# First attention of a four-layer kernel on one core: probabilities made with keys on partitions, the maximum alone by query

## The chip, the cores and the metric

One core of a Trainium2 chip runs the whole program in one launch. The metric is the device time of a launch in microseconds (us), the median of the runs shown. The engines have queues of their own and meet by semaphores: PE (matrix products, which land in PSUM, eight banks of 512 float32 per partition), DVE (vector work), ACT (activations and copies), POOL (GpSimd) and SP (issues most of the DMAs).

## What is computed

Four blocks in a row on x of 4 x 1024 x 256, each added to x behind a gate: a cross attention, a mixture of 16 experts, a second attention, and a quantised linear layer. The change is in the first block alone:

```python
def _L0_xattn_ref(q_in, mem, mem_mask, Wq, Wk, Wv, Wo):
    q = _split_heads(q_in @ Wq.T)          # 16 heads of 16
    k = _split_heads(mem @ Wk.T)           # 64 keys for each of 4 batches
    v = _split_heads(mem @ Wv.T)
    scores = jnp.einsum('bhqd,bhkd->bhqk', q, k) / jnp.sqrt(jnp.float32(D_HEAD))
    scores = jnp.where(mem_mask, scores, -jnp.inf)
    attn = jax.nn.softmax(scores, axis=-1)
    out = jnp.einsum('bhqk,bhkd->bhqd', attn, v)
    ...
    return out @ Wo.T

x = x + jnp.tanh(g_xattn[0]) * _L0_xattn_ref(_layernorm(x, axis=-1), ctx_1024, mask_Bx1x1xS2_bf1, ...)
```

## The kernel before

The program has stages, with a barrier between them. A setup stage loads x (4 MB, kept in SBUF as `x_sb`) and the weights, makes the keys of all batches (`kT_sb`), spreads them to `kbd`, where the keys of eight heads stand beside each other with zeros for the other heads' rows, and the values to `vbd`.

The first attention then runs over eight chunks of 512 queries (two per batch), each of four tiles of 128 queries. In a chunk PE transposes the normalised x (`x0`, `x1`), makes the queries in two halves of 128 rows (`q0`, `q1`), and the scores of each tile: 128 queries by 16 heads times 64 keys, 1024 columns in two PSUM banks. The mask is added there by a one-pass bf16 product (L651) before the float32 product (L653). DVE takes the maximum over the keys (L574) and subtracts it (L576) into `probs` in SBUF; ACT takes the exponential (L521); DVE sums it (L582) and takes the reciprocal (L585); POOL multiplies (L474). PE transposes the probabilities back, so that keys lie on partitions: eight pairs of heads `pt0` to `pt7` (L661), which ACT moves to `probT`. Then come the values (L679, four products of 32 columns at a time, each in its own 32 columns of PE's array), whose result `oT` ACT moves, and the output projection (L689), which DVE adds to x (L591).

The chunks are software pipelined: beside the probabilities of chunk c PE makes the queries and scores of chunk c + 1, in an order written out by hand in `body`. Every engine executes its own list in order. Scores use banks 0 to 3, two for each tile in turn. Everything else goes through a ring of banks 4 to 7: a product may start when the product four places earlier in the ring has been moved out (`Ring.free`). Beside the attention the weights of two experts per chunk are loaded and split into a high part (ACT, L506 and L507) and a low part (DVE, L563 and L565) for the next stage. `ln_vector` (L215 to L227) normalises chunk c + 2 ahead.

## Time and profile before

| what | value |
|---|---|
| median of 3 runs | 1526.14 us (1525.16 to 1529.63) |
| span of the profiled execution | 1543.6 us |
| own time of the profiled execution beside it | only its span is given, 17.5 us above the median of the runs |
| busy: PE, DVE, ACT, POOL | 1113.8, 1014.9, 637.1, 486.5 us |
| mean granted PE clock | 0.848 of 2.4 GHz |
| setup / first attention / all that follows | 0 to 27.65 / 27.65 to 241.65 / 241.65 to 1543.6 us |

Busy time is what an engine's instructions cover; the shares over the whole span mix stages with different limits, so a change in one stage is read from that stage's own stretch of the trace. Idle time is put down to what released the engine.

### The profile page before, as it was taken

The numbers are of one execution on the slowest core, as the hardware profiler recorded it, in microseconds if no ns is written. First come the engines' busy times: TensorE is split into PE (matmuls) and PEld (weight loads), VectorE is DVE, ScalarE is ACT, GpSimd is POOL, SyncE is SP. The second block draws the span as 40 slices with busy tenths as digits, with TensorE's granted clock in tenths as the row PEclk, the third lists the DMA queues.
The fourth block names the chain that finished last, engine by engine and source line by source line (L and its number), as shares of the span: only waits on it lengthen the run. The fifth ranks groups of instructions, "written<-read, shape, count | busy, mean of one in ns | idle before, by whom it ended". The sixth has DMA issues, their size and how long they took to land. (4 is left out here: it accounts for less than half of the span.)

```text
span 1543.6 us, 23798 instructions
## 1 busy us (share of the span) xinstructions
PE 1113.8 (72%) x8155; PEld 569.9 (37%) x8155; DVE 1014.9 (66%) x1856; ACT 637.1 (41%) x1280; POOL 486.5 (32%) x539
## 2 busy tenths in 40 slices
PE   3799985342407999805465568999999999998757
PEld 2355553121204666502232323333333333331646
DVE  4899985455453766525556387888888888870665
ACT  0455553111102333201122207777677767775430
POOL 1243341767760000078777061111111111111110
PEclk7999997656657999956767759999999999995988
DMA  6001100222259999943656431111211121100003
GB/s 204 22 21 42 41 1 14 89 85 86 91 200 214 250 258 259 244 122 89 210 182 196 143 101 40 55 38 39 59 54 38 39 59 53 38 2 1 1 0 109
DMA packets 183649, 146.24 MB, mean 95 GB/s; under 512 B 102638, under 2 KB 160494, under 8 KB 183546
## 3 DMA queue, kind: packets, MB, share of 16 engines
q1 hardware_dynamic: 162570, 102.61, 25.3%
q0 software_dynamic: 12288, 33.57, 6.7%
q10 hardware_dynamic: 8688, 8.66, 1.7%
q8 instruction: 68, 1.11, 0.3%
q14 instruction: 35, 0.29, 0.1%
HBM read 53.11 MB, written 68.55 MB: 79 GB/s over the span
## 5 line engine op out<-in xcount | busy, mean ns | idle before, releaser
L1782 DVE TENSOR_REDUCE small<-ps 128x2 f32<-128x960 f32 (+6 forms) x384 | 379.0, 1040 | 56.8 <-PE ps L1837 56.5
L1761 ACT ACTIVATE region<-ps 128x512 f32<-128x512 f32 (+5 forms) x768 | 343.1, 532 | 110.0 <-PE ps L1851 108.6
L1732 POOL TENSOR_SCALAR_AFFINE_SELECT region<-region 128x512 f32<-128x512 f32 (+2 forms) x160 | 87.7, 548 | 427.4 <-ACT region L1761 427.4
L1851 PE MATMUL ps<-region 50*128 50x512 f16 (+5 forms) x896 | 198.6, 332 | 26.7 <-ACT region L1761 23.7
L1927 PE MATMUL ps<-region 128*32 128x512 f32 (+5 forms) x1792 | 192.9, 504 | 2.0 <-POOL region L1732 1.5
L1200 PE MATMUL ps<-region 128*128 128x384 f16 x696 | 125.2, 331 | 38.8 <-DMA region<-expert_rows 38.0
L859 POOL DMA_INDIRECT expert_rows<-region,small x128 | 130.6, 1020 | 65.1 <-issue 36.6
L1837 PE MATMUL ps<-region 48*128 48x480 f16 (+6 forms) x896 | 141.4, 333 | 13.5 <-DVE small L1782 11.3
L1365 POOL DMA_INDIRECT region<-result_rows,home x128 | 133.5, 1043 | 38.0 <-issue 36.8
L1851 PEld LDWEIGHTS ps<-region 50*128 50x128 f16 (+1 forms) x896 | 54.2, 95 | 211.3 <-ACT region L1761 195.6
L1200 PEld LDWEIGHTS ps<-region 128*128 x696 | 67.6, 99 | 83.5 <-issue 45.5
L474 POOL TENSOR_TENSOR region<-region,small 128x1024 f32<-128x1024 f32 x32 | 61.0, 1917 | 118.4 <-DVE small L585 118.4
L1523 PE MATMUL ps<-region 128*128 128x512 f16 (+1 forms) x240 | 62.7, 435 | 42.0 <-DVE region L1462 32.8
L1436 DVE SCALAR_TENSOR_TENSOR x_sb<-region,weights,x_sb 128x256 f32<-128x256 f32 x128 | 52.1, 477 | 52.4 <-DMA region<-result_rows,home 52.4
L1082 DVE SCALAR_TENSOR_TENSOR region<-ps,region 128x384 f32<-128x384 f32 x58 | 32.3, 558 | 74.4 <-ACT region L902 74.3
L1832 PE MATMUL ps<-small 64*128 64x128 bf16 (+1 forms) x768 | 68.8, 245 | 17.0 <-POOL small L1713 11.9
L902 ACT ACTIVATE region<-ps 128x384 f32<-128x384 f32 x58 | 28.5, 491 | 122.2 <-PE ps L1200 122.2
L1213 PE MATMUL ps<-region 128*128 x522 | 67.4, 275 | 2.5 <-DVE region L1094 2.5
L1837 PEld LDWEIGHTS ps<-region 48*128 48x128 f16 x896 | 49.1, 97 | 51.3 <-DVE small L1782 47.2
L653 PE MATMUL ps<-region,small 128*128 128x512 f32 x128 | 65.4, 592 | 0.0
L1353 POOL MEMSET small<- 128x1 f32 x1 | 0.1, 101 | 204.0 <-POOLq L778 204.0
L1094 DVE COPY region<-ps 128x768 f32<-128x768 f32 x58 | 55.0, 947 | 3.4 <-PE ps L1213 3.4
(237 smaller groups left out, 1693.3 us busy)
## 6 DMA issues: line engine op xcount, KB each, us to landing
result_rows<-region SPq DMA_DIRECT2D x58, 384.0 KB, 4.1
region<-v_parts SPq DMA_DIRECT2D x16, 576.0 KB, 4.1
v_parts<-region SPq DMA_DIRECT2D x14, 576.0 KB
region<-k_parts SPq DMA_DIRECT2D x96, 68.0 KB, 2.2
region<-q_parts SPq DMA_DIRECT2D x96, 64.0 KB, 2.1
k_parts<-region SPq DMA_DIRECT2D x16, 272.0 KB
x_sb<-in_x ACTq DMA_DIRECT2D x8, 512.0 KB, 9.1
region<-in_w13T SPq DMA_DIRECT2D x16, 256.0 KB, 3.0
```

The costliest lines, as they stand in the source:

```text
L653: ins = nc.tensor.matmul(o, qT[:, m, j * P:(j + 1) * P], kbd[:, m, bass.ds(b, 1), :].rearrange("p a n -> p (a n)"), start=False, stop=True)
L859: nc.gpsimd.indirect_dma_start(out=xs, out_offset=bass.IndirectOffsetOnAxis(ap=sloti[:, b, at_:at_ + 1], axis=0), in_=rows[:, b, j, :], in ...
L1200: ins = nc.tensor.matmul(ps[:, 2 * (g % DEEP) + half_, 0:GROUP], w, xgT[:, g % G_BUFS, part, kh, :], start=n == 0, stop=n == 5)
L1213: ins = nc.tensor.matmul(ps[:, 6 + j // 2, (j % 2) * D:(j % 2 + 1) * D], (hgh, hgl)[part][:, g % DEEP, j * P:(j + 1) * P], flat((w2h, w2l) ...
L1365: nc.gpsimd.indirect_dma_start(out=yg[c % 2][:, j, r, :], out_offset=None, in_=ys, in_offset=bass.IndirectOffsetOnAxis(ap=home[:, c, at_:a ...
L1732: nc.gpsimd.affine_select(out=t, in_=t, compare_op=ALU.is_ge, fill=0.0, base=r0, pattern=[[0, G], [1, w]], channel_multiplier=-1).then_inc ...
L1761: nc.scalar.activation(dst, src, ACT.Exp, scale=SCALE).then_inc(s_exp, 1)
L1782: nc.vector.tensor_reduce(nmp[:, qt, :, p0:p0 + np_, place], s_pair(n + first)[:, :, 0:np_ * nk] .rearrange("p e (h k) -> p e h k", h=np_) ...
L1832: nc.tensor.matmul(o, mask_id[rows[half], part, :], mask_dg[rows[half], part, 0:np_, :], start=part == 0, stop=False, skip_group_check=True)
L1837: ins = nc.tensor.matmul(banks[half][:, p * nk:(p + 1) * nk], q_of(r, v)[:, p0 + p, qt * P:(qt + 1) * P], k_of(r, v)[:, p0 + p, k0:k0 + nk ...
L1851: ins = nc.tensor.matmul(o, k_of(rr, tbuf)[:, pair, kt * P:kt * P + rows], q_of(rr, tbuf)[:, pair, q0:q0 + nq], start=True, stop=True)
L1927: ins = nc.tensor.matmul(ps[32 * h:32 * h + 32, O_BANK, q0 - hf * CH:q0 - hf * CH + nq], vg[0:rows, buf, (kt * G + h) * 32:(kt * G + h + 1 ...
```

## The change

The probabilities are no longer made by query and transposed. The scores by query stay, without a mask, and serve the maximum alone (`largest`). The masked-out keys are replaced by the mean of the kept ones in the setup, so that they can't raise the maximum. The negated maximum is cut into two bf16 parts (`shift_parts`), transposed by PE (`shifts`, the product `n`) and moved by ACT to `negT`. Then PE makes the scores a second time with keys on partitions (`scores_by_key`): for each of eight pairs of heads one bf16 product that spreads the shift over the 128 keys of the pair, and one float32 product of 32 rows of keys with 32 rows of queries on top. Four pairs use the four groups of 32 rows of the array and four banks. ACT takes the exponential out of PSUM straight to `probT`, with the mask as its bias. After the values, PE sums the probabilities over the keys (`row_sums`), DVE takes the reciprocal of all 512 sums of 16 heads at once (a 128x256 tile), PE spreads it over the head's 16 rows (`spread_out`), and DVE multiplies the output with it (`normalise`). POOL's multiplication and the transposes of probabilities are gone. `Turns` replaces `Ring`: one list of 20 products a chunk over the same four banks, the same rule of four places. POOL makes the constants for this in the setup.

The core of the diff:

```diff
-                order.mark(nc.vector.memset(maskb[:], 0.0))
...
+                order.mark(nc.vector.tensor_tensor(kT_sb[:], ps[:, 0:KH, 0:B * CTX],
+                                                   keep[:].unsqueeze(1).to_broadcast([P, KH, B * CTX]), ALU.mult))
+                order.wait()
+                order.mark(nc.vector.tensor_reduce(mean[:], kT_sb[:].rearrange("p m (b k) -> p m b k", b=B), AX.X, ALU.add))
...
+                st = [((f"st{a}", c), "act") for a in range(PAIRS_OF)]
+                tail = [(("ov0", c), "act"), (("ov1", c), "act"), (("sum", c), "dve"), (("r0", c), "dve"), (("r1", c), "dve"),
+                        (("o0", c), "dve"), (("o1", c), "dve")]
+                return x + st[0:4] + q[0:1] + st[4:8] + q[1:2] + tail + ([(("n", c + 1), "act")] if ahead else [])
...
+                def exp(c, a):
+                    act.wait_ge(s_full, turns.full((f"st{a}", c)))
+                    nc.scalar.activation(probT[:, a, :], ps[:, turns.bank((f"st{a}", c)), :], ACT.Exp, scale=SCALE,
+                                         bias=mbias[:, c // 2:c // 2 + 1]).then_inc(s_act, 1)
...
-                    nc.vector.tensor_tensor(probs[h][:, j, :].rearrange("p (h k) -> p h k", k=CTX), s3,
-                                            nmx[:, j, :].unsqueeze(2).to_broadcast([P, H, CTX]),
-                                            ALU.add).then_inc(s_shift, 1)
...
+                def reciprocals(c):
+                    dve.wait_ge(s_full, turns.full(("sum", c)))
+                    nc.vector.reciprocal(recip[:], ps[:, turns.bank(("sum", c)), 0:QH]).then_inc(s_dve, 1)
+
+                def normalise(c, m):
+                    dve.wait_ge(s_act, turns.moved((f"ov{m}", c))[1])
+                    dve.wait_ge(s_full, turns.full((f"r{m}", c)))
+                    nc.vector.tensor_tensor(oT[:, m, :], ps[:, turns.bank((f"r{m}", c)), :], oT[:, m, :], ALU.mult).then_inc(s_dve, 1)
...
+                def scores_by_key(c, pairs):
+
+                    wait_moved("n", c)
                     for a in pairs:
...
+                        m, r = a // 4, slice(32 * (a % 4), 32 * (a % 4) + 32)
+                        wait_free(f"st{a}", c)
+                        nc.tensor.matmul(slot(f"st{a}", c), shift_of[r, m, :], negT[r, :], start=True, stop=False)
+                    for a in pairs:
+                        m, g = a // 4, a % 4
+                        r = slice(32 * g, 32 * g + 32)
+                        nc.tensor.matmul(slot(f"st{a}", c), kbd[r, m, c // 2, P * g:P * g + P], qT[r, m, :],
+                                         start=False, stop=True).then_inc(s_full, 1)
...
+                def row_sums(c):
+
+                    wait_free("sum", c)
+                    for g in range(4):
+                        for m in range(KH):
+                            for qh in range(2):
+                                k = 2 * m + qh
+                                ins = nc.tensor.matmul(slot("sum", c)[32 * k:32 * k + 32, 0:QH], sum_of[:, g, :],
+                                                       probT[:, 4 * m + g, qh * QH:(qh + 1) * QH], start=g == 0, stop=g == 3)
...
+                    scores_by_key(c, range(4))
+                    if ahead:
+                        queries(c + 1, 0)
+                    scores_by_key(c, range(4, 8))
+                    if ahead:
+                        queries(c + 1, 1)
+                    if ahead:
+                        scores(c + 1, 0)
+                        scores(c + 1, 1)
+                    values(c, 0)
+                    values(c, 1)
+                    row_sums(c)
+                    if ahead:
+                        scores(c + 1, 2)
+                    spread_out(c, 0)
+                    spread_out(c, 1)
+                    if ahead:
+                        scores(c + 1, 3)
+                    outputs(c)
+                    if ahead:
+                        shifts(c + 1)
```

PE's list for the middle of a chunk before, from the queries of the next chunk on (L642 queries, L661 transposed probabilities, L651 and L653 mask and scores; what an instruction waits for stands in brackets):

```order
L642 MATMUL ps<-small 128x512 [waits a_act_moved,a_dve_moved]
L642 MATMUL ps<-small 128x512
L642 MATMUL ps<-small 128x512 [waits a_dve_moved]
L642 MATMUL ps<-small 128x512
L661 MATMUL ps<-ident,region 128x128 [waits a_prob,a_act_moved]
L661 MATMUL ps<-ident,region 128x128 [waits a_prob] x3
L661 MATMUL ps<-ident,region 128x128 [waits a_act_moved]
L661 MATMUL ps<-ident,region 128x128 x3
L651 MATMUL ps<-maskb,onesb 128x512 [waits a_shifted,a_act_moved]
L653 MATMUL ps<-region,small 128x512
```

The two halves of the queries follow each other, and eight transposes stand between the second half and the first scores. Now, in the same place of a chunk (L756 shift products, L760 key products, L728 query halves, L738 scores):

```order
L756 MATMUL ps<-region 128x512 [waits a_act_moved] x3
L760 MATMUL ps<-small,region 128x512 x4
L728 MATMUL ps<-small 128x512 [waits a_act_moved]
L728 MATMUL ps<-small 128x512
L756 MATMUL ps<-region 128x512 [waits a_act_moved] x4
L760 MATMUL ps<-small,region 128x512 x4
L728 MATMUL ps<-small 128x512 [waits a_act_moved]
L728 MATMUL ps<-small 128x512
L738 MATMUL ps<-region,small 128x512 [waits a_maxed,a_act_moved]
```

The query halves stand apart, each behind a group of key products, and every group, half and the first scores begin with a wait for a move by ACT. DVE's list for one chunk, between the low parts of the expert weights and the additions to x, before:

```order
L574 TENSOR_REDUCE small<-ps 128x16
L576 TENSOR_TENSOR region<-ps,small 128x1024
L582 TENSOR_REDUCE small<-region 128x16
L585 RECIPROCAL small<-small 128x16
L574 TENSOR_REDUCE small<-ps 128x16
```

and now:

```order
L639 TENSOR_REDUCE small<-ps 128x16 [waits a_scores] x2
L657 RECIPROCAL region<-ps 128x256 [waits a_bank_full]
L639 TENSOR_REDUCE small<-ps 128x16 [waits a_scores]
L662 TENSOR_TENSOR small<-ps,small 128x512 [waits a_bank_full,a_act_moved] x2
L639 TENSOR_REDUCE small<-ps 128x16 [waits a_scores]
L648 CAST region<-small 128x2x4x2 [waits a_maxed]
```

Of the three instructions on a whole tile one is left; the reciprocal of the chunk's sums and the two products with it have come between the maxima. After the last chunk, the low parts of two experts now stand behind the additions to x instead of ahead of them.

## Rows read from the trace of the kernel before

**Rows 1.** Busy times by stage: stretch, its length, busy PE, PEld, DVE, ACT, POOL, clock, DMA.
```profile
27.65:61.86 34.21, 21.08 (x52) 9.72 (x53) 24.65 (x48) 8.61 (x13) 11.52 (x13) 0.75 0.19 58
61.86:227.28 165.42, 153.38 (x721) 90.74 (x719) 147.92 (x233) 93.32 (x156) 59.06 (x38) 1.00 0.10 29
227.28:241.65 14.37, 11.49 (x61) 8.94 (x61) 4.64 (x7) 5.87 (x10) 1.32 (x1) 0.77 0.00 1
```

**Rows 2.** The same view, one chunk of the seven.
```profile
85.21:108.89 23.68, 22.07 (x105) 13.12 (x104) 21.61 (x36) 13.25 (x22) 8.58 (x6) 1.00 0.11 34
```

**Rows 3.** Groups by line, 37 to 232 us: count, busy us, mean ns of one.
```profile
L576 DVE TENSOR_TENSOR region<-ps,small 128x1024 f32<-128x1024 f32 x32 | 39.2, 1224 | 1.1
L574 DVE TENSOR_REDUCE small<-ps 128x16 f32<-128x1024 f32 x32 | 39.0, 1218 | 9.8 <-PE ps L653 9.6
L582 DVE TENSOR_REDUCE small<-region 128x16 f32<-128x1024 f32 x32 | 38.3, 1197 | 0.0
L563 DVE SCALAR_TENSOR_TENSOR region<-region 128x512 f16<-128x512 f32 x17 | 13.4, 790 | 5.4 <-ACT region L507 5.4
...
L565 DVE SCALAR_TENSOR_TENSOR region<-region 128x256 f16<-128x256 f32 x17 | 8.8, 518 | 0.0
...
L585 DVE RECIPROCAL small<-small 128x16 f32<-128x16 f32 x32 | 8.1, 253 | 1.1
```

**Rows 4.** PE's timeline in one chunk: start us, busy us of the merged instructions, line.
```profile
108.37 3.70 PE L642 MATMUL ps<-small 128*128 128x512 f32 x8 [1.60 <-DVE x_sb L591]
111.91 1.04 PE L661 MATMUL ps<-ident,region 128*128 128x128 f32 x8
112.78 0.38 PE L651 MATMUL ps<-maskb,onesb 128*128 128x512 bf16 x1
113.00 1.02 PE L653 MATMUL ps<-region,small 128*128 128x512 f32 x2
113.86 0.38 PE L651 MATMUL ps<-maskb,onesb 128*128 128x512 bf16 x1
...
121.94 1.93 PE L679 MATMUL ps<-region,small 128*32 128x512 f32 x16
123.80 0.39 PE L651 MATMUL ps<-maskb,onesb 128*128 128x512 bf16 x1
```

**Rows 5.** Timeline: moves by ACT in the first, a middle and the last chunk.
```profile
40.57 0.60 ACT L511 ACTIVATE small<-ps 128x512 f32<-128x512 f32 x1 [1.66 <-PE ps L642]
...
110.39 0.60 ACT L511 ACTIVATE small<-ps 128x512 f32<-128x512 f32 x1 [2.94 <-PE ps L642]
...
118.92 2.04 ACT L511 ACTIVATE region<-ps 128x512 f32<-128x512 f32 x4
...
236.49 0.60 ACT L511 ACTIVATE small<-ps 128x512 f32<-128x512 f32 x1 [0.29 <-PE ps L679]
...
237.13 3.72 PE L689 MATMUL ps<-small 128*128 128x256 f32 x16 [0.71 <-ACT small L511]
```

**Rows 6.** PE's timeline in the second attention: two products of 50 rows, and one.
```profile
1010.05 0.39 PE L1851 MATMUL ps<-region 50*128 50x512 f16 x2
...
1011.19 0.39 PE L1851 MATMUL ps<-region 50*128 50x512 f16 x1 [0.20 <-ACT region L1761]
```

**Rows 7.** Groups by line over the whole span, other stages.
```profile
L2003 ACT ACTIVATE region<-ps,gambet 128x512 f32<-128x512 f32 x16 | 11.7, 774 | 30.0 <-PE ps L2092 30.0
...
L1807 DVE TENSOR_TENSOR region<-ps,small 128x512 f32 x14 | 9.7, 691 | 2.0 <-DVE small L1805 0.2
...
L1805 DVE RECIPROCAL small<-ps 128x32 f32<-128x32 f32 x16 | 5.7, 358 | 48.1 <-PE ps L1887 48.1
```

**Rows 8.** DVE's timeline in the setup.
```profile
18.45 1.70 DVE L372 CAST maskb<-small 1x256 bf16<-1x256 f32 x8
```

**Rows 9.** Busy times in the last chunk, columns as in rows 1.
```profile
223.60:227.00 3.40, 1.10 (x7) 0.68 (x5) 3.33 (x6) 2.49 (x5) 2.16 (x2) 1.00 0.00 0
227.00:230.40 3.40, 1.90 (x9) 1.74 (x9) 3.40 (x5) 0.98 (x2) 1.60 (x1) 0.50 0.00 0
```

More of the change, by code:

```diff
@@ L112, in free, with __init__, bank, full @@
         return e, c * self.by.count(e) + self.moved_before[e] - self.previous[at:].count(e) + 1
+class Turns:
+    def __init__(self, items, banks):
+        self.place = {key: i for i, (key, _) in enumerate(items)}
+        assert len(self.place) == len(items)
+        self.by = [e for _, e in items]
+        seen = {}
+        self.counted = []
+        for e in self.by:
+            seen[e] = seen.get(e, 0) + 1
+            self.counted.append(seen[e])
+        self.banks = banks
+    def bank(self, key):
+        return self.banks[self.place[key] % len(self.banks)]
+    def full(self, key):
+        return self.place[key] + 1
+    def moved(self, key):
+        i = self.place[key]
+        return self.by[i], self.counted[i]
+    def free(self, key):
+        i = self.place[key] - len(self.banks)
+        return (self.by[i], self.counted[i]) if i >= 0 else None
 def hold(eng, sem, n, tick):
@@ L397, in flamingo @@
         oT = view(small, "oT", [P, KH, CH], F32)
[L398 to L401 removed]
+        nmx = view(small, "nmx", [P, TC, KH, 4, 2], F32)
         junk = view(small, "junk", [P, 4], F32)
@@ L495, in _ @@
                                         pattern=[[1, P]], channel_multiplier=-1).then_inc(s_const, 1)
-                normalise(0, 0)
-                chunks(pool, body)
+                for c in range(CHUNKS - 2):
+                    ln_pool(nc.gpsimd, c + 2, s_var, s_rstd)
             @block.scalar
             def _(act):
-                credit(nc.scalar.activation(junk[:, 1:2], half[:, 0:1], ACT.Copy), s_act, CREDIT)
                 def high(k, at_, n):
@@ L543, in _, with move @@
-                move_queries(ring_first, 0)
-                for j in range(TC):
-                    exp(0, 0, j)
-                high(*SHARED)
-                chunks(act, body)
-                for expert in experts_beside(1, B - 1):
-                    high(*expert)
-                move_probs(ring_last, 0)
-                move_outputs(ring_last, 0)
+                def move(name, c, dst):
+                    act.wait_ge(s_full, turns.full((name, c)))
+                    nc.scalar.activation(dst, ps[:, turns.bank((name, c)), :], ACT.Copy).then_inc(s_act, 1)
@@ L592, in add @@
                                                        in1=xt, op0=ALU.mult, op1=ALU.add).then_inc(s_dve, 1)
-                def softmax(c, h, order):
-                    shift(c, h, 0, order)
-                    for j in range(1, TC):
-                        shift(c, h, j, order)
-                        row_sum(c, h, j - 1, order)
-                    row_sum(c, h, TC - 1, order)
-                FIRST, EACH = 2 * LN_MARKS + 2 * TC, LN_MARKS + 2 * TC
-                def body(c, h, b, b_next, more):
-                    order = Order(dve, s_self, c * EACH + FIRST)
-                    if more:
-                        ln_vector(nc.vector, order, c + 2, 1e-5, s_var, s_rstd, s_xn, free=(s_full, ring.full(c, "x1")))
-                    for expert in experts_beside(h, b):
-                        low(expert)
-                    softmax(c + 1, 1 - h, order)
-                    add(ring, c, c)
@@ L617, in _ @@
+                shift_parts(0)
                 low(SHARED, signal=False)
-                chunks(dve, body)
-                for expert in experts_beside(1, B - 1):
+                for c in range(CHUNKS):
+                    ahead = c + 1 < CHUNKS
+                    if c + 2 < CHUNKS:
+                        ln_vector(nc.vector, order, c + 2, 1e-5, s_var, s_rstd, s_xn, free=(s_full, turns.full(("x1", c + 1))))
+                    if c:
+                        for expert in experts_beside((c - 1) % 2, (c - 1) // 2):
+                            low(expert)
+                    if ahead:
+                        largest(c + 1, 0)
+                        largest(c + 1, 1)
+                    reciprocals(c)
+                    if ahead:
+                        largest(c + 1, 2)
+                    normalise(c, 0)
+                    normalise(c, 1)
+                    if ahead:
+                        largest(c + 1, 3)
+                        shift_parts(c + 1)
+                    add(c)
@@ L709, in _ @@
-                queries_of(pe_first, 0, 0)
-                pe_first.wait_moved(0, "q1")
-                for j in range(TC):
-                    scores(0, 0, j)
-                chunks(eng, body)
-                transposed_probs(pe_last, 0, CHUNKS - 1, 1)
-                values(pe_last, 0)
-                outputs(pe_last, 0)
+                        ins.then_inc(s_full, 1)
+                transposed(0)
+                for m in range(KH):
+                    queries(0, m)
+                for j in range(TC):
+                    scores(0, j)
```

340 lines of the change are left out of this document (186 added, 154 removed).

## The prediction

> **What bounds the kernel now.** I read the busy times by stage first. The change touches the setup, up to 27.65 us, and the first attention, 27.65 to 241.65 us [rows 1]; the other 1302 us run the same code. In the attention's middle, 61.86 to 227.28 us, PE is busy 153.4 of 165.4 us and DVE 147.9: both are nearly full, ACT and POOL are not. Cut into chunks, that stretch is seven periods, nearly all of 23.68 us [rows 2].
>
> Then I read the groups by line. The three DVE instructions on a whole 128x1024 tile cost 1.2 us each [rows 3], four of each per chunk: 4 x (1.22 + 1.22 + 1.20) = 14.6 us, with normalisation, split weights and the rest making up the 21.6 us of DVE in a chunk [rows 2].
>
> Then PE's timeline for one chunk, where distances between starts say what an instruction costs the queue [rows 4]. Eight 128-column transposes take 112.78 - 111.91 = 0.87 us. A 512-column product of one-pass bf16 takes 113.00 - 112.78 = 0.22, and a float32 one, issued as two passes, 113.86 - 113.00 = 0.86. Eight float32 products of 32 columns each take 123.80 - 121.94 = 1.86, not 8 x 0.86: four run side by side, so two rounds are 1.72, and 0.14 is left for changing the array's division. A chunk's PE work before is then 0.87 (x) + 3.44 (queries) + 3.48 (32 transposes of probabilities) + 1.73 (mask) + 6.88 (scores) + 1.72 (values) + 3.44 (outputs) = 21.6 us.
>
> **The change: work.** DVE loses L576 and L582 with their small reciprocals, 4 x (1.22 + 1.20 + 0.25) = 10.7 us a chunk [rows 3]. It gains a reciprocal of 128x256, which no row shows. Sixteen columns take 0.253 us [rows 3] and 32 take 0.358 [rows 7], so 6.6 ns a column: 0.358 + 224 x 0.0066 = 1.83 us (bounds: 0.36 if width were free, 2.9 in proportion). It gains two 128x512 products from PSUM at 0.69 [rows 7] and eight 16-element instructions, taken as 0.85 us together (bounds 0.4 to 2.0, eight at 0.25). DVE falls to about 15 of 23.7 us. POOL's 1.9 us normalisations go too. ACT keeps about its load: eight moves and four 1024-wide exponentials become eight 512-wide exponentials. Each reads its bias from a tile: with two such operands an ACTIVATE takes 0.774 us against 0.60 [rows 5, 7], so one adds 0.09.
>
> PE loses 3.48 + 1.73 = 5.2 us a chunk and gains four bf16 transposes (0.25), two groups of four shift and four key products, row sums (32 passes of 256 columns, four side by side: 1.72) and spreading (four float32 products of 256 columns: 1.72). The groups use 32 of the 128 rows. Two tiles of 50 rows do run side by side: two 512-column products take 0.39 us, as one does [rows 6]. So I take four as one, 0.22 + 0.86 a group; no row shows four. Sum 0.25 + 2.16 + 1.72 + 1.72 = 5.85: **PE does not get lighter, it goes from 21.6 to 22.2 us a chunk.**
>
> The Trainium skill, TensorE: Matmul & The Clock Gate, Part 3 (Packing small matmuls), measures only 3.07 times for four tiles of 32 rows and 512 columns. My estimate from that page: 0.33 us more a group, 0.65 a chunk, 5 us in all; the sum would be 1564 instead of 1559.
>
> **The change: order.** This decides. PE executes strictly in the written order, and the new ring hands each of banks 4 to 7 on after four products: the first query half needs the bank of st0, the fourth shift of the second group needs that query half moved, the second query half needs st4's bank. None of these has other PE work in front of it. The turnarounds come from the rows: from the end of a product's issue to ACT's start 0.30 (108.37 + 1.72 to 110.39) [rows 4, 5]; to DVE taken the same; an ACT move 0.60 and 0.04 more until PE starts (236.49 + 0.60 to 237.13); back-to-back moves 0.48 apart (four in 2.04) [rows 5].
>
> One chunk, from the end of issue of the shift transposes (0): shift moved and both x moved by ACT, 0.30 + 2 x 0.48 + 0.64 = 1.90; fourth shift and key products +1.08 = 2.98; exponential of st0 +0.30 + 0.73 = 4.01; first query half +0.14 + 1.72 = 5.87; moved +0.94 = 6.81; fourth shift and key products +1.08 = 7.89; exponential of st4 +1.03 = 8.92; second query half +1.86 = 10.78; moved +0.94 = 11.72; two scores +3.44 = 15.16; values and row sums +0.14 + 3.44 = 18.74; reciprocal +0.30 + 1.83 = 20.87 (a score lies beside it); spreading +1.72 = 22.6; the last score +1.72 = 24.3; outputs +3.44 = 27.8; next shift transposes +0.25 = **28.0 us against 23.68**. PE waits some 5.7 us of it. The last maximum and the parts of the shift (1.2 + 0.85) and both normalisations hide behind outputs and score; without that cover they would cost up to 2.4.
>
> **Ends of the stage.** In setup the mask's casts (1.70 [rows 8]) and two more instructions go; means, masking of keys and eight small instructions come: +1.6 us on DVE's path (bounds 0 to 4). POOL's 24 small instructions lie beside it, and the two extra loads on SP's queue are small and needed late; uncovered they would cost 2 us. Chunk 0's queries were moved at 41.17 [rows 5]; now 42.8, four scores 6.9, last maximum 1.5, parts 0.85, transposes 0.25: the first chunk starts at 52.3. Seven periods: 248.3. The last chunk has no next one beside it: shift 0.94, first group 1.08, four exponentials 2.8, second group 1.08, four exponentials 2.8, second values 1.0, row sums 1.72, reciprocal 2.13, spreading 1.72, normalising 1.0, outputs 3.44, add 1.1, and now behind it DVE's halves of two experts (0.79 + 0.52 each [rows 3], those overlapping, so 2 x 1.1): 23.0. End at 271.3 instead of 241.65: **+30 us**. For the first and last chunk's clock (below) I add 3, as an estimate between 0 and 7: **+33**.
>
> This is summed on the profiled execution (span 1543.6 us, 17.5 above the runs' median of 1526.14) and carried over unscaled; 1.1% of 33 does not matter. **Forecast 1559 us.** A measurement of this kernel can tell about 0.3% (4.6 us) from no change.
>
> **The rivals.**
> - **No side-by-side for four tiles.** For it: only two tiles are seen, in 16-bit types. Against: eight-pass groups of four column tiles work in float32. Each group's key products would be 3.43 us; the first exponential starts under them, so the query half moves from 4.01 to 5.6: +1.6 a group, 3.2 a chunk, with the ends 24: 1583.
> - **PE's clock falls in the chunks.** In the last chunk before, PE was busy 1.1 us in 223.6 to 227.0, and the next stretch ran at 0.50, the level of 1.2 GHz [rows 9]. Now the stretches 0 to 4 and 5.9 to 8.9 of every chunk hold about 2 and 1.1 us of PE issue. Against: a wait of 1.60 us in each chunk before [rows 4] left it at 1.00 [rows 2]. If one query half and a group in most chunks run at half speed, +3 each, +21: 1580.
> - **Faster: PE's waits vanish, its work bounds.** If other work covered every hand-over between PE and ACT, the period would be PE's 22.2, and the stage would end at 52.3 + 155.4 + 23.0 = 230.7, 11 us earlier: 1515. It decides where a period falls under (241.65 - 52.3 - 23.0) / 7 = 23.8 us, so where 4.2 of the 5.7 us of waits are covered. For it: DVE, the other full engine, is relieved. Against: the written order has nothing to put there.
> - **Nothing.** With 1.5 us of wait a chunk instead of 5.7 the period is 23.8 and the time 1526; nothing in the rows points there.
>
> **How the numbers follow.** Forecast 0.66, no side-by-side 0.11, clock 0.14, faster 0.05, nothing 0.04. Slower is the sum of the first three, 0.91. The forecast's own range is 1541 (small unknowns at their low ends, clock full) to 1573. The range reaches to the two slower rivals: 1541 to 1584; left out are the last two cases and the upper tails, together under 0.2.
>
> **What would show it.** Right: periods of 28 us; DVE about 60% busy and waiting for PE; PE waiting about 1 us before each query half, fourth shift and first score, released by ACT; reciprocal near 1.8. Wrong: periods under 24; four key products over 3 us apart; a reciprocal that PE does not wait for; a clock below 1.0 in the chunks.

## The result, and the profile after

| kernel | median of the runs (us) | range |
|---|---|---|
| before | 1525.65, 4 runs | 1523.53 to 1529.63 |
| after | 1560.12, 4 runs | 1558.95 to 1560.95 |

The ratio is 1.0228, with a 95% interval of 1.0202 to 1.0254: slower, by 34.5 us, where 33 were forecast. The profiled execution of after took 1558.95 us, its span 1557.1.

The whole program's busy times of after, from its page:

```profile
PE 1130.9 (73%) x8379; PEld 561.6 (36%) x8379; DVE 962.3 (62%) x1850; ACT 613.8 (39%) x1255; POOL 427.3 (27%) x527
```

DVE is busy 53 us less than before. PE is busy 17 us longer, which is no measure of its work: after's busy time in a chunk, 24.9 us, exceeds the whole period of the reordered run (below), which has the same products. The stages answer to [rows 1, 2]. Busy times by stretch, with the columns of rows 1: the setup, the start, a middle chunk, the last one, and all behind the stage:

```profile
0.00:34.95 34.95, 7.23 (x40) 5.18 (x40) 11.52 (x43) 1.49 (x2) 10.62 (x38) 0.74 0.54 170
34.95:58.75 23.80, 16.38 (x36) 7.18 (x37) 12.70 (x40) 3.21 (x6) 3.28 (x8) 0.73 0.28 84
141.02:168.44 27.42, 24.89 (x135) 12.40 (x133) 15.39 (x35) 10.45 (x19) 1.01 (x1) 1.00 0.09 29
250.70:276.40 25.70, 17.62 (x100) 8.25 (x97) 9.13 (x14) 8.28 (x15) 0.00 (x0) 0.80 0.00 1
276.40:1557.10 1280.70, 915.49 (x7283) 454.16 (x7283) 826.44 (x1532) 527.68 (x1099) 407.38 (x475) 0.84 0.38 104
```

Every one of the seven chunks takes 27.42 us, where a chunk took 23.68. DVE's share of it is 15.4 us. The stage ends at 276.40 instead of 241.65: +34.75, close to the timed 34.5 (+33.7 against the second profile of before, which ends it at 242.74). One thing does not fit: what follows the stage took 1280.7 us here and 1302 in the profile of before, with the same code. A second profile of before settles that.

### The profile page after: what moved, and what is told of

Read it like the earlier page. It is cut to its first block and busy times, and to the rows that moved or that the text cites. A ratio compares the mean times of both kernels' runs of the same rounds, so it can differ in the third digit from the quotient of the medians.

```text
span 1557.1 us, 24292 instructions
## 1 busy us (share of the span) xinstructions
PE 1130.9 (73%) x8379; PEld 561.6 (36%) x8379; DVE 962.3 (62%) x1850; ACT 613.8 (39%) x1255; POOL 427.3 (27%) x527
## 3 DMA queue, kind: packets, MB, share of 16 engines
q1 hardware_dynamic: 163256, 102.64, 25.1%
## 5 line engine op out<-in xcount | busy, mean ns | idle before, releaser
L1482 POOL DMA_INDIRECT region<-result_rows,home x128 | 129.7, 1013 | 38.0 <-issue 36.3
L265 POOL TENSOR_TENSOR rstd<-ve,half 128x4 f32<-128x4 f32 x24 | 24.6, 1026 | 221.1 <-DVE ve L255 203.4
L639 DVE TENSOR_REDUCE small<-ps 128x16 f32<-128x1024 f32 x32 | 39.2, 1224 | 67.4 <-PE ps L738 66.5
L738 PE MATMUL ps<-region,small 128*128 128x512 f32 x128 | 60.1, 604 | 5.5 <-ACT small L583 5.5
```

The source lines that it names most:

```text
L1482: nc.gpsimd.indirect_dma_start(out=yg[c % 2][:, j, r, :], out_offset=None, in_=ys, in_offset=bass.IndirectOffsetOnAxis(ap=home[:, c, at_:a ...
```

## The experiments

All stage ends and periods in this section are read from the traces: a period is the distance between the starts of two chunks' output products, the end is that of the last DVE instruction of the stage.

| kernel | period | stage end | median us | ratio to before (95%) |
|---|---|---|---|---|
| before, second profile | 23.68 | 242.7 | 1524.45, 16 runs | |
| after | 27.42 | 276.4 | 1560.12 | 1.0228 (1.0202 to 1.0254) |
| no column loads | 27.42 | 275.6 | 1557.58 | 1.0244 (1.0184 to 1.0303) |
| maximum from upper halves | 24.20 | 251.2 | 1535.06 | 1.0081 (1.0045 to 1.0116) |
| reordered | 23.83 | 250.0 | 1532.17 | 1.0063 (1.0036 to 1.0090) |
| other setup | 27.42 | 265.6 | 1549.11 | 1.0184 (1.0127 to 1.0241) |
| all together | 22.00 | 225.9 | 1504.85 | 0.9872 (0.9816 to 0.9927) |
| one more chunk in flight | 20.94 | 218.4 | 1502.63 | 0.9867 (0.9813 to 0.9920) |
| the same, scores ahead of outputs | 20.86 | 218.3 | 1503.23 | 0.9882 (0.9821 to 0.9944) |
| before with its gates late | 23.68 | 238.0 | 1518.46 | 0.9975 (0.9943 to 1.0007) |

Each ratio is taken to runs of before made in the same session, whose medians were 1524.45 (16 runs), 1525.91 (7 runs: other setup, all together, one more chunk) and 1524.03 us (13 runs: the last two rows); it isn't the quotient of the medians shown.

For every kernel the median, less the stage end and the 1.9 us by which a run exceeds its span, leaves 1277 to 1283 us for what follows the stage (1277 in all together), so the stage explains the differences to within some 3 us. Single executions spread more there (1270 to 1283 in these profiles), which is why the medians are compared.

### Before, profiled again

No edit.

> The kernel before once more, for a second profile of it. The changed kernel's attention stage ends 34.7 us later than in the first profile of before (276.4 against 241.65 us), its runs are 34.5 us longer at the median, but its profile is only some 13.5 us longer. Theory: the stage alone grew, and the first profile of before spent about 20 us too many behind the stage; then the stage ends at 241 to 242 us again, what follows it takes 1281 us (plus or minus 4) instead of 1302, and the span is 1522 to 1526 us. Rival: the change also made something behind the stage 20 us faster; then what follows the stage takes about 1302 us again.

Measured: span 1525.5, run 1527.28 us. Busy times of this second execution of before, columns as in rows 1:

```profile
242.74:1525.50 1282.76, 912.74 (x7283) 453.81 (x7283) 826.31 (x1532) 527.58 (x1099) 408.52 (x475) 0.84 0.38 104
```

What follows the stage takes 1282.8 us, the 1281 of the theory within its 4 us. The change touched the first attention and the setup alone; the 1302 us of the first profile were that one execution's.

### The mask's column loads

```diff
-                for dup in range(2):
-                    sp.dma_start(mcol[64 * dup:64 * dup + CTX, :], mask.rearrange("b s -> s b"),
-                                 allow_slow_non_contiguous=True).then_inc(s_mask, 16)
-                dve.wait_ge(s_mask, 48)
+                dve.wait_ge(s_mask, 16)
-                nc.vector.tensor_scalar(mbias[:], mcol, -1.0, 3.0e38, ALU.add, ALU.mult)
+                nc.vector.memset(mbias[:], 0.0)
```

The setup of after is 7.3 us longer than before's. SP's issues in it, from the timeline (start, time to issue, line, target):

```profile
2.87 1.41 SPq L346 DMA_DIRECT2D small<-in_mask  x2
4.31 3.06 SPq L349 DMA_DIRECT2D small<-in_wqT  x1
```

In before the same weight took 0.39 us to issue:

```profile
2.76 0.39 SPq L303 DMA_DIRECT2D small<-in_wqT  x1
```

ACT's timeline, its eight loads of x, in after and then in the second profile of before:

```profile
3.26 18.06 ACTq L362 DMA_DIRECT2D x_sb<-in_x  x8
```

```profile
3.25 12.61 ACTq L316 DMA_DIRECT2D x_sb<-in_x  x8
```

The DMA view of after up to 35 us: the first line is the rate in 40 slices of 0.875 us, then two groups of loads with their size and the time from issue to landing:

```profile
GB/s 0 0 3 120 272 279 329 79 9 5 28 145 191 207 82 165 273 315 379 384 365 346 349 349 348 351 345 349 289 241 117 70 0 0 0 0 0 0 0 0
...
small<-in_wqT SPq DMA_DIRECT2D x1, 256.0 KB, 13.1
...
small<-in_mask SPq DMA_DIRECT2D x2, 0.2 KB, 10.8
```

Right behind the mask's loads the rate falls from 329 to 5 GB/s. The Tanh on ACT stands behind the loads of x, and DVE's whole chain behind the Tanh: it starts at 22.88 instead of 17.43. The column loads move 4 bytes in each of 64 partitions, twice.

> The changed kernel without the two column loads of the mask (one byte per partition); the bias of the exponentials is set to zero by a memset instead, so the mask's bias is left out. Theory (these two loads hold up the queues in the first 20 us, so that the x tiles and the weights come late): DVE's chain over the keys starts 5.4 us earlier, near 17.5 us instead of 22.9, the first chunk starts 5.5 us earlier, and the time falls by 5.5 us to 1554.6. Rival A (the row of the mask sent to all partitions is what blocks): no change, 1560. Rival B (the start is bound by TensorE at half clock, not by DVE): the chain starts earlier but the first chunk moves by less than 1.5 us, 1559.

Measured: 1557.58 us, 2.5 less than after. DVE's first instruction, the first chunk's transposes, and a stretch of busy times (columns as in rows 1), from three views of this run:

```profile
19.56 0.40 DVE L439 TENSOR_SCALAR boutb<-boutb,tg 128x256 f32<-128x256 f32 x1 [19.56 <-ACT tg L362]
```

```profile
55.06 1.04 PE L718 MATMUL ps<-ident,xn 128*128 128x128 f32 x8
```

```profile
57.80:61.20 3.40, 2.86 (x10) 0.84 (x3) 1.38 (x4) 2.21 (x4) 0.85 (x1) 0.50 0.00 0
```

Neither theory nor rival alone. The two column loads are 3.3 of the 5.4 us (22.88 to 19.56). The other 2.1 us are left when only the row sent to 128 partitions remains: the loads of x now take 14.74 us to issue, and 12.68 when that row goes too (the other setup, below). The rate still falls, from 310 to 91 GB/s, in the same slices. The profiles' counts of packets on the largest queue, which carries the loads that SP issues, agree: 163256 in after, 162712 here, 162570 in before, so the column loads are 544 packets and the row 142.

The first chunk begins 3.7 us earlier (58.75 to 55.06), but the stage ends only 0.8 us earlier. From the first chunk's start to its outputs it took 26.49 us, in after 23.75: here PE's clock stood at 0.50 in part of it, where after had 1.00. So 2.7 of the 3.7 us were lost in the first chunk, at the lower clock. These readings rest on the traces: the medians lie only 2.5 us apart, and the runs of the two kernels overlap.

### The maximum from half the bits

```diff
-nc.tensor.matmul(ps[...], qT[:, m, j * P:(j + 1) * P], kbd[:, m, c // 2, :],
+nc.tensor.matmul(ps[...], qT_top[:, m, j * P:(j + 1) * P], kbd_top[:, m, c // 2, :],
+        kbd_top = kbd[:].bitcast(BF16).rearrange("p m b (k two) -> p m b k two", two=2)[:, :, :, :, 1]
```

`qT_top` is the same view of `qT`. Only the maximum sees these scores; it is subtracted in the exponent and divided out again, so it need not be the exact one.

> The changed kernel with the scores for the maximum made from the upper halves of the F32 numbers, read as BF16: one pass through TensorE instead of four, 0.43 us instead of 1.71 for each of the four pairs of a chunk, 5.1 us of TensorE's work a chunk; the other products keep all their bits. Theory (the chain of handovers sets the period): the two pairs ahead of the values lie on the chain (-2.6 us), the third lies beside the reciprocal and gains nothing, the fourth gives 0.5 us until the normalising ends; period 27.42 - 3.1 = 24.3 us, first chunk's start 2 us earlier, last chunk unchanged, time 1560 - 7 x 3.1 - 2 = 1536. Rival A (TensorE's own work of 24.9 us, as its busy row says, sets the period): -5.1 us a chunk, period 22.3, time 1522. Rival B (reading every second BF16 costs as much as the passes saved): 1560.

Measured: period 24.20 (theory 24.3), 1535.06 us (theory 1536). PE's timeline of a chunk from its first two pairs of scores (L740) on:

```profile
166.27 1.08 PE L740 MATMUL ps<-region,small 128*128 128x512 bf16 x4 [0.69 <-ACT small L585]
167.28 1.92 PE L770 MATMUL ps<-region 128*32 128x512 f32 x16
169.02 1.91 PE L781 MATMUL ps<-region 128*32 128x256 f32 x32
...
172.90 1.96 PE L790 MATMUL ps<-region 128*128 128x256 f32 x8 [1.41 <-DVE region L659]
...
175.72 0.48 PE L800 MATMUL ps<-small 128*128 128x256 f32 x1 [0.40 <-DVE small L664]
```

The chain forecast each pair. The first two take 167.28 - 166.27 = 1.01 us where after spends 3.63 (below): -2.6. The third gives nothing: from row sums to spreading it is 172.90 - 169.02 = 3.88 us, to the hundredth as in after (161.25 - 157.37), only that PE now waits 1.41 us for the reciprocal where it had a score to do. The fourth gives 0.7: from spreading to outputs it is 175.72 - 172.90 = 2.82 us, in after 3.52. Of 5.1 us of work removed, 3.2 came out of the period: a path, not a sum of work. The period shows this, not the total, in which the ends moved too. The first chunk began 3.6 us earlier (2 were forecast) and needed the same 23.7 us to its outputs, at a clock of 0.50 to begin with. The last chunk, from the outputs before it to its own, took 20.35 us instead of 22.97, where no change was forecast.

### The same instructions, reordered

```diff
-                    if ahead:
-                        transposed(c + 1)
+                    if ahead:
+                        scores(c + 1, 0)
                     scores_by_key(c, range(4))
-                    if ahead:
-                        queries(c + 1, 0)
+                    if ahead:
+                        scores(c + 1, 1)
                     scores_by_key(c, range(4, 8))
-                        queries(c + 1, 1)
-                        scores(c + 1, 0)
-                        scores(c + 1, 1)
+                        scores(c + 1, 2)
                     values(c, 0)
                     values(c, 1)
                     row_sums(c)
                     if ahead:
-                        scores(c + 1, 2)
+                        scores(c + 1, 3)
+                    if further:
+                        transposed(c + 2)
                     spread_out(c, 0)
                     spread_out(c, 1)
-                    if ahead:
-                        scores(c + 1, 3)
+                    if further:
+                        queries(c + 2, 0)
+                        queries(c + 2, 1)
                     outputs(c)
```

ACT's and DVE's lists and the ring follow; a second buffer holds the queries made a chunk earlier.

> The changed kernel with all its instructions, in another order on TensorE: the queries of a chunk are made a chunk earlier into a second buffer, and the four pairs of scores for the maximum stand where TensorE waits: one behind the transposes of the shift, one behind each group of key products, one behind the row sums, and the next transposes and queries beside the reciprocal and the normalising. Theory (the period of 27.42 us is 22.2 us of work and 5.2 us of waits for ACT and DVE): all but some 0.8 us of the waits are covered, period 23.0 us; the first part is 5 us longer (a second set of queries ahead of chunk 0), six periods of 23.0, a seventh without queries of 18.7 and a last chunk of 22 us put the stage's end at 63.8 + 138 + 18.7 + 22 = 242.5 us, time 1526. Rival A (TensorE's work is the 24.9 us that its busy row shows): period 25 us, stage end 256, time 1539. Rival B (ACT or DVE sets the pace): period 27, time 1560 or more.

Measured: period 23.83, 1532.17 us. Busy times of a middle chunk, then, from PE's timeline, its two key groups (L752 shifts, L756 keys) and the scores (L734) behind each:

```profile
151.42:175.24 23.82, 23.63 (x133) 12.38 (x132) 15.22 (x34) 10.56 (x19) 1.00 (x2) 1.00 0.11 34
```

```profile
156.96 0.40 PE L752 MATMUL ps<-region 32*128 32x512 bf16 x4
157.19 1.03 PE L756 MATMUL ps<-small,region 32*128 32x512 f32 x8
158.14 1.99 PE L734 MATMUL ps<-region 128*128 128x512 f32 x4
160.06 0.46 PE L752 MATMUL ps<-region 32*128 32x512 bf16 x3
160.72 0.39 PE L752 MATMUL ps<-region 32*128 32x512 bf16 x1 [0.19 <-ACT region L592]
...
161.89 1.98 PE L734 MATMUL ps<-region 128*128 128x512 f32 x4
```

Not an instruction fewer, and 3.6 us less a chunk: at least that much of the 27.42 us was waiting. PE is now busy 23.63 of 23.82 us, with one visible wait of 0.19. But its busy row can't be read as work: in after it showed 24.89, more than this whole period, and so rival A's reading of it falls. Starts tell more. The first key group takes 158.14 - 156.96 = 1.18 us, the second, with its wait, 161.89 - 160.06 = 1.83. So some 0.65 us is waiting and about 23.2 are work, an estimate. The theory holds in its mechanism, and its work term of 22.2 was too small: a group takes 1.18 where 1.08 were taken, a pair of scores 1.82 to 1.92 (158.14 to 160.06, the next product being one of 32 rows) where 1.72 were, the row sums 1.84 for 1.72. The stage ends at 250.0, not at 242.5. This order alone did not beat before, whose period was 23.68.

### Another setup

```diff
-                sp.dma_start(mrow, mask.rearrange("b s -> (b s)").partition_broadcast(P)).then_inc(s_mask, 16)
+                sp.dma_start(mrow[0:1, :], mask.rearrange("b s -> (b s)").unsqueeze(0)).then_inc(s_mask, 16)
+                nc.tensor.matmul(ps[:, 6, 0:B * CTX], onesb[:], mask0[:], start=True, stop=True).then_inc(s_all, 1)
-                dve.wait_ge(s_gate, 5 * 16 + 1)
-                order.mark(nc.vector.tensor_scalar(boutb[:], boutb[:], tg[:, 1:2], None, ALU.mult))
...
+                order.mark(nc.vector.tensor_copy(keep[:], ps[:, 6, 0:B * CTX]))
...
+                dve.wait_ge(s_gate, 5 * 16 + 1)
+                order.mark(nc.vector.tensor_scalar(boutb[:], boutb[:], tg[:, 1:2], None, ALU.mult))
```

`mask0` holds the mask's row in its first partition and zeros elsewhere. The excerpt leaves out the bias column and POOL's selects that were moved.

> The changed kernel with another setup and the same chunks: the mask is loaded as one row into one partition (as before the change) and sent to all partitions by one product with ones on TensorE, the bias column is cut out of it on VectorE, VectorE begins with the keys instead of waiting for the gates' Tanh, and 12 of POOL's 20 selects stand in the attention stage. Theory (the setup is bound by VectorE's chain, which the mask loads made late): the chain of VectorE starts near 9 us instead of 22.9, the setup ends with the last x tile at some 23.3 us instead of 35.0, and the stage ends 11.7 us earlier; time 1560 - 11.7 = 1548. Rival A (as the run without the column loads suggests, what the start gains is given back by TensorE at half clock in the first chunks): the setup ends 11.7 us earlier, but the stage only some 8, time 1552. Rival B (x loads bound the start): setup end at 28 or later, 1554.

Measured: 1549.11 us (theory 1548), stage end 265.6, 10.8 us earlier. From DVE's timeline: its start, the spreading of the keys, and the first normalisation:

```profile
6.68 0.28 DVE L426 CAST small<-small 1x256 bf16<-1x256 uint8 x1 [5.62 <-DMA small<-in_mask]
...
15.42 6.37 DVE L452 TENSOR_SCALAR region<-small 128x256 f32<-128x256 f32 x16 [1.25 <-POOL small L383]
...
26.17 1.41 DVE L248 BATCH_NORM_STATS2 stats<-x_sb 128x6 f32<-128x256 f32 x4
```

The loads of x take 12.68 us to issue again, as before. The setup ends at 26.1, not 23.3: the sixteen products of L452 waited 1.25 us for POOL and take 6.37 us beside POOL's selects, where the same ones took 4.29 in before. So the time met its forecast more closely than the mechanism did, which was luck. Of the 10.8 us the setup gave 8.85 (34.95 to 26.1), the stretch ahead of the first chunk 0.6, and the last chunk 1.4, where spreading was busy 1.96 us at a clock of 1.00 instead of 3.34. The clock did not take this gain back, and gave a little.

### All together

The three edits above in one kernel.

> Everything together: the order of the reordering run, the maximum from upper halves, and the other setup. With short pairs of scores the waits come back in part: by the reordering run's rows 5.8 us less work a chunk, and about 4.3 us of new waits (0.4 behind the shift, 2.0 behind the first key group for the exponentials, 1.0 behind the second, 0.9 beside the reciprocal), so the theory (waits for ACT and VectorE are what is left) gives a period of 22.3 us, stage end near 232 us, time 1514. Rival (work alone): period 18 us, time 1488.

Measured: period 22.00 (theory 22.3), 1504.85 us: the waits came back where the short scores no longer cover them. Two of them, in the values (L780) and ahead of the spreading (L802):

```profile
145.25 1.06 PE L780 MATMUL ps<-region 128*32 128x512 f32 x8 [0.76 <-ACT region L608]
...
150.00 1.97 PE L802 MATMUL ps<-region 128*128 128x256 f32 x8 [0.53 <-DVE region L670]
```

The time is 9 us lower than the theory's 1514. The stage ends 6 us earlier than forecast (225.9 for 232), 2 of them in the seven periods; the other 3 us lie behind the stage, and where these came from was not traced. The medians of this kernel and the next two lie 1.2 to 1.3% below before's, with intervals that end below 1.

### One more chunk in flight

```diff
                     scores_by_key(c, range(4))
+                    if c:
+                        outputs(c - 1)
                     scores_by_key(c, range(4, 8))
                     if c + 1 < CHUNKS:
                         scores(c + 1, 2)
+                        scores(c + 1, 3)
+                    if c + 2 < CHUNKS:
+                        both(c + 2)
                     values(c, 0)
                     values(c, 1)
                     row_sums(c)
-                        scores(c + 1, 3)
-                        transposed(c + 2)
+                        transposed(c + 3)
+                        shifts(c + 1)
+                        scores(c + 2, 0)
+                        scores(c + 2, 1)
                     spread_out(c, 0)
                     spread_out(c, 1)
```

`both` makes the two query halves.

> As the run before it, but with one more chunk in flight: the outputs of a chunk stand between the next chunk's two key groups, the queries of the chunk after the next behind the second group, and transposes, shift and the first two pairs of scores beside the reciprocal, so that each of the waits has 2 to 3.5 us of work in it. Theory (waits covered, 18.2 us of work left): period 18.5 to 19 us, a longer first part, stage end near 208 us, time 1490. Rival A (VectorE's 15.2 us with its own waits, or ACT, now sets the pace): period 20 to 21, time 1502. Rival B (the longer first part at half clock takes it all back): time as in the run before, 1514.

Measured: period 20.94 (theory 18.5 to 19), 1502.63 us (theory 1490): the number of rival A. ACT's and DVE's lists follow the new order; DVE normalises the next x ahead of a chunk's additions. The timeline around the outputs (L831), with DVE's normalisation (L260) and additions (L693):

```profile
116.29 3.69 PE L831 MATMUL ps<-small 128*128 128x256 f32 x16 [0.75 <-ACT region L613]
...
118.42 1.38 DVE L260 TENSOR_SCALAR xn<-x_sb,mv,rstd 128x256 f32<-128x256 f32 x4 [1.12 <-POOL rstd L265]
119.72 1.40 DVE L693 SCALAR_TENSOR_TENSOR x_sb<-ps,tg,x_sb 128x512 f32<-128x512 f32 x2
120.52 0.39 PE L787 MATMUL ps<-region 32*128 32x512 bf16 x1 [0.22 <-DVE x_sb L693]
```

DVE is busy only 15.0 of 20.94 us. The outputs wait for the exponentials to leave a bank, the shifts of the second key group for the additions to leave theirs (0.22 and another 0.27 us). But the additions themselves start right behind a normalisation that waited 1.12 us for POOL's statistics, which is part of rival A's reason. Which of these hand-overs sets the period, this run does not show. Against the run before, the stage is 7.4 us shorter but the median only 2.2 us: with four or five runs each, and ratios whose intervals overlap, these two can't be told apart.

### Scores ahead of the outputs, and a control

The deeper order with `scores(c + 1, 2)` and `scores(c + 1, 3)` moved to ahead of `outputs(c - 1)`:

> The deeper order with one step moved: the second two pairs of scores for the maximum stand ahead of the outputs instead of behind the second key group. Theory (in the run before, the outputs waited 0.75 us for the exponentials' banks and the second group 0.49 us for the additions): the 0.84 us of scores cover the first and push back the second; period 20.94 - 1.2 = 19.7 us, time 1502.6 - 7 x 1.2 = 1494. Rival (VectorE, with 15.2 us of work and a wait for the statistics of POOL, sets the period): period stays at 20.5 to 21, time 1502.

Measured: period 20.86 (theory 19.7), 1503.23 us (theory 1494): a miss, and the rival's number. The outputs wait no longer, and the wait has gone to the next product that needs a bank of the exponentials, the queries:

```profile
142.60 0.70 PE L759 MATMUL ps<-small 128*128 128x512 f32 x1 [0.66 <-ACT region L613]
```

The additions again start right behind a normalisation that waited 1.12 us for POOL, so the rival's reason, DVE with its wait, is not ruled out. No run moved the normalisation.

The control is the kernel before with the three scalings by the gates at the end of DVE's setup list:

```diff
-                dve.wait_ge(s_gate, 5 * 16 + 1)
-                order.mark(nc.vector.tensor_scalar(boutb[:], boutb[:], tg[:, 1:2], None, ALU.mult))
...
+                dve.wait_ge(s_gate, 5 * 16 + 1)
+                order.mark(nc.vector.tensor_scalar(boutb[:], boutb[:], tg[:, 1:2], None, ALU.mult))
```

> The kernel before with one edit to its setup: VectorE makes keys and values first and the three scalings by the gates last, so that it no longer waits for the Tanh behind ScalarE's eight loads of x. A control: how much of what the other setup gives belongs to any version. Theory: VectorE starts at some 7 us, waits for the keys until 11 us, and the setup ends near 24.5 us instead of 27.7; time 3 us less than before, 1523. Rival (the clock of the first chunks or the x loads take it back): 1526.

Measured: 1518.46 against 1524.03 us, 5.6 us where 3 were forecast, with an interval that still holds 1, and a stage end at 238.0 instead of 242.7. DVE starts at 6.81 and then waits for POOL ahead of the spreading of the keys:

```profile
15.77 4.29 DVE L376 TENSOR_SCALAR region<-small 128x256 f32<-128x256 f32 x16 [4.01 <-POOL small L338]
```

Against this control the three best kernels are 14 to 16 us faster; the one timed in the same session is 15.2 us faster. How much of that belongs to the new form (cheaper maxima, fewer DVE passes) and how much to the better order stays open: no run gave before's own chunks, in which PE is busy 22.07 of 23.68 us [rows 2], another order.

## Why the prediction was right

Sign and size held: 1560.1 us against 1559. Step by step, the end of the stage comes out of the forecast's 271.3 as + 6.45 (first chunk at 58.75 instead of 52.3) - 4.06 (seven periods shorter by 0.58) + 2.7 (last chunk 25.7 instead of 23.0) = 276.4. The two ends were 9.15 us too low, 3 us had been set aside for the clock, and the periods were 4.06 too high. That these nearly cancel, so that the total is 1.1 us off, is luck; the sum was better than its terms. The sign and the greater part of the size are not: seven periods longer by 3.74 us are 26 us of the 34.75.

**The period: right, 27.42 for 28.0.** The chain can be laid beside PE's and ACT's timeline of after, from the transposes of x on:

```profile
141.02 1.04 PE L721 MATMUL ps<-ident,xn 128*128 128x128 f32 x8
...
144.75 1.98 PE L728 MATMUL ps<-small 128*128 128x512 f32 x4 [0.66 <-ACT region L591]
...
147.43 0.39 PE L756 MATMUL ps<-region 32*128 32x512 bf16 x1 [0.37 <-ACT small L583]
147.43 1.24 PE L760 MATMUL ps<-small,region 32*128 32x512 f32 x8
...
148.59 2.42 ACT L591 ACTIVATE region<-ps,region 128x512 f32<-128x512 f32 x4 [1.21 <-PE ps L760]
...
149.32 1.98 PE L728 MATMUL ps<-small 128*128 128x512 f32 x4 [0.66 <-ACT region L591]
...
152.00 3.70 PE L738 MATMUL ps<-region,small 128*128 128x512 f32 x8 [0.69 <-ACT small L583]
155.63 1.92 PE L768 MATMUL ps<-region 128*32 128x512 f32 x16
...
157.37 1.91 PE L779 MATMUL ps<-region 128*32 128x256 f32 x32
...
159.34 1.76 DVE L657 RECIPROCAL region<-ps 128x256 f32<-128x256 f32 x1 [2.39 <-PE ps L779]
...
161.25 1.97 PE L788 MATMUL ps<-region 128*128 128x256 f32 x8
...
164.77 3.62 PE L798 MATMUL ps<-small 128*128 128x256 f32 x16
```

Counted from 141.02: the first query half starts at 3.73 (forecast 4.01), the fourth shift of the second group at 6.41 (6.81), the second query half at 8.30 (8.92), the scores at 10.98 (11.72), the spreading at 20.23 (20.87), the outputs at 23.75 (24.3). PE waits at each of the places named, released by ACT. All of the difference is made by the first score, 0.74 us; the steps behind it took 0.16 more than forecast. From the fourth shift to the exponential it takes 148.59 - 147.43 = 1.16 where 1.08 + 0.30 were taken, because the key products start under the shift products, twice; and the 0.14 for changing the array's division is not seen ahead of either query half.

**PE's waits and work: the split was off, the sum not.** 22.2 us of work and 5.7 of waits were forecast. By the reordering run about 23.2 us are work, if the same products cost the same in after; that leaves some 4.2 us of waits. Work was undersized at the pairs of scores, the groups and the row sums by 1 us, waits oversized by 1.5.

**DVE and the reciprocal: right.** 15.4 us for 15, the reciprocal 1.76 for 1.83, the normalising products 0.69.

**Four products side by side: right.** In the reordering run four float32 key products of 0.86 us each take 158.14 - 157.19 = 0.95. That is at least 3.6 products at a time, and the rival without side-by-side would have shown over 3 us. By the factor of 3.07 in the Trainium skill (TensorE: Matmul & The Clock Gate, Part 3) the four would have taken 1.12 us, an estimate. Here the measurement decides.

**The setup: the step that failed.** It says of the mask's column loads: "the two extra loads on SP's queue are small and needed late; uncovered they would cost 2 us." They were priced by when their data is needed. They cost by what stands behind them: weights, x, and the Tanh on which DVE's chain waits. The setup grew by 7.3 us instead of 1.6. The column loads account for 3.3 at DVE's start, the row sent to all partitions for the other 2.1, DVE's own new instructions for 1.8 (1.6 forecast). The 5.7 us by which the setup outgrew its forecast and 0.7 us at the first queries, which took 7.41 us instead of 6.7 at a clock of 0.59, are the 6.45 by which the first chunk was late. That 0.7 is not the change's: in the second profile of before they took 7.34.

**The clock: right for after.** The seven chunks stayed at 1.00, against the rival. It is not assured: in the runs without the column loads and with the short scores the first chunk had stretches at 0.50. The clock of the last chunk did fall, as before's had [rows 9]. Busy times of after in it, columns as in rows 1:

```profile
252.40:255.80 3.40, 2.04 (x12) 0.69 (x12) 0.91 (x2) 2.42 (x4) 0.00 (x0) 1.00 0.00 0
255.80:259.20 3.40, 2.86 (x16) 0.20 (x8) 0.00 (x0) 2.40 (x4) 0.00 (x0) 0.53 0.00 0
259.20:262.60 3.40, 3.40 (x28) 1.36 (x28) 0.00 (x0) 1.86 (x5) 0.00 (x0) 0.50 0.03 5
```

In the first stretch PE was busy 2.04 of 3.40 us, waiting for exponentials with no next chunk to fill in; in the next it was granted about half its clock, 1.2 GHz. The last chunk's later products in PE's timeline:

```profile
261.04 2.80 PE L779 MATMUL ps<-region 128*32 128x256 f32 x32
...
265.81 3.34 PE L788 MATMUL ps<-region 128*128 128x256 f32 x8 [1.97 <-DVE region L657]
...
270.01 3.72 PE L798 MATMUL ps<-small 128*128 128x256 f32 x16 [0.85 <-DVE small L662]
```

Counted from 250.70, the row sums start at 10.34 (forecast 9.7), the spreading at 15.11 (13.55), the outputs at 19.31 (16.27), and the chunk ends at 25.70 (23.0). So 2.1 of the 2.7 us lie behind the start of the row sums. From row sums to spreading it is 4.77 us where the middle chunk took 3.88, from spreading to outputs 4.20 where it took 3.52 with a pair of scores between; the row sums ran in a stretch granted 0.50, the spreading in one granted 0.54. The 3 us set aside were for both ends.

**The faster rival: wrong for this order, in part right for another.** It asked for other work to cover the waits. The reordering run supplied it and reached 1532, not 1515. Some 11 of these 17 us are seven periods of 23.83 instead of 22.2, whose work is 23 us and more; the rest lies in the ends.

## What to carry to other kernels

Moving work from a loaded engine pays only as far as the path through the others gets shorter: lay each step's hand-over end to end in the written order before counting busy time. A product that only steers (a maximum that is divided out again) can be made from fewer bits at once. And price a small load by the queue behind it, not by its bytes.

## What the runs showed of the hardware that was not expected

- Two loads of 256 single bytes, behind a row sent to 128 partitions, took the DMA rate from 329 to 5 GB/s and kept it under 80 for some 3 us; they landed after 10.8 us. A weight of 256 KB behind them landed after 13.1 us, without them after 7.4. Sending the mask's 256 bytes to all 128 partitions, 32 KB, was not free either: without the column loads the rate still fell to 91 GB/s, and DVE still started 2.1 us late. The Trainium skill (DMA: Bandwidth & Descriptors, Rules for kernel authors) says that a last dimension which isn't contiguous becomes one descriptor for each element. The packet counts agree: the two column loads are 544 packets, 272 for each 256 bytes. Why the row sent to all partitions is slow, no run shows.
- A float32 tile read as every second bf16 runs at about one-pass speed: two such pairs of scores, four 512-column products, took 1.01 us from start to start, the change to products of 32 columns included, beside 4 x 0.22 for packed bf16 [rows 4].
- DVE's sixteen products of 256 columns took 6.37 us beside POOL's selects, eight of which took 5.29 us instead of 4.35, and 4.29 without them. The Trainium skill (SBUF — State Buffer, SBUF: two separate sides) tells of a port pair that a DVE instruction in a 2-port mode, or one with two SBUF inputs, and a POOL instruction lock against each other for a whole instruction. The trace agrees in direction, but in which mode DVE ran nothing here shows, and no run took the selects away alone.
